# Adapter-conditioned attention with a routed low-rank layer: factor rows taken from the values' products, the last query groups crossed, first outputs in halves

## The chip, the cores and the metric
The kernel runs on one core of one Trainium2 chip. The metric is the device time of one execution in microseconds. Three runs of the kernel before gave a median of 1053.36 us (1052.51 to 1054.79).

## What is computed
`x` has 8 batches of 256 tokens with 1024 features, all in float32. Each layer of the reference adds two terms:

```python
h = x @ W.T + b + 2.0 * (x @ lora_A[a]) @ lora_B[a]      # a: one adapter per batch, rank 16
q, k, v = h @ w_q, h @ w_k, h @ w_v                      # 32 query heads, 8 key/value heads, 32 wide
o = softmax(q k^T / sqrt(32)) v                          # within a batch
x = x + o @ w_o
y = x @ weight[c].T                                      # c: one of 8 matrices per batch
logits = y @ router_w.T                                  # 4 experts, the best 2 kept, softmax
x = x + sum_e gate_e * 4.0 * (y @ A[e].T) @ B[e].T       # rank 16
```

## The kernel before, in words
Every float32 product is done as three fp32r products: each operand is split into a high part (ScalarE copies and rounds it) and a low part (VectorE subtracts), and high x high, high x low and low x high are added up in PSUM. So a `matmul` over k = 0..7 (1024 features in `KT` = 8 tiles) is 24 products.

**Fold** (`fold_stage`). `W` and `w_q`, `w_k`, `w_v` are multiplied into one matrix `wq` of twelve blocks of 128 columns (`BLOCKS`), in three chunks `j` of four blocks, and likewise `lora_B` (into `bp`, stored to DRAM as `b_scratch`) and the bias (`brow`). VectorE and ScalarE evacuate a chunk's eight tiles, split the next chunk's eight rows of `Wqkv` (`split_q`), and only then evacuate `bp`, on whose bank tile 6 of the next chunk waits.

**Attend** (`attend_stage`). Batches go in four pairs p of 512 tokens. A pair has 16 steps, one for each key/value group g = 0..7 and each batch c; N = 64 steps in all, and the work of step n is spread over steps n to n+3. In TensorE's step the order is: scores 0 and 1, **first slot** of projection products, outputs of n-3, transpose of the maxima of n-1 (`turn`), transposed scores 0 and 1 of n-2, scores 2 and 3, **second slot**, transposed scores 2 and 3 of n-2. The two slots are filled by the list `WORK`: entry s is (first slot, second slot); "q3:4-8" is k = 4 to 7 of query group 3, "+" means the next pair. The units alternate between two PSUM banks in the order `SEQ`: unit i may start (`free`) when unit i-2 has been evacuated, that is when ScalarE has written its high and VectorE its low part. VectorE finds each step's row maxima (four per step), splits them, and SP copies them as two rows into `q_stack` for the transposed scores two steps on. ScalarE takes the exponentials (four per step), GpSimd adds their halves (`p_sum`), and the outputs wait for both. Each engine and SP's DMA queue works strictly in the order written out in its `step` function.

The unit "u" is the factor h A of both batches (`project_u`): per k and batch one product with 64 weight columns and one with 32, 32 products of 256 columns a pair. It needs all of the next pair's x, so x is loaded in steps 11 and 12 as soon as q7, the last reader, lets its tiles go (`x_used`); the splits follow on ScalarE in steps 11 and 12 and on VectorE in 12 and 13. The values' units v0 to v3 (one per 128 tokens) have x as weights and 256 columns of `wq` moving, and end with one low-rank product.

**Finish** (`finish_stage`). Per batch: eight tiles `w_o_tile` of o W_o (24 products of 256 columns), `residual` on VectorE, eight rows `cond_row` (six products of 512 columns) that fold the conditional matrix into the router and A, and the gated low-rank part. What is possible is done ahead, in the last pair's steps and after (s = n - LAST, s = 0..18): `WO_LOAD` and `WO_SPLIT` load and split W_o, `load_o(0)` (nine DMAs: eight broadcast rows of reciprocal sums and o) is issued by SP in s = 8, `normalise` and `scale_lo` make o(0)'s parts on VectorE in s = 10 and 11, `FIRST_TILES` puts the eight tiles of batch 0 in the slots from the second of s = 12 on, and `ROWS_MULT` rows 0 to 4 from the second slot of s = 16 on. Rows 5 to 7, o(1)'s normalisation and tile 0 of batch 1 come in `first()`. The low part of row r needs its high part, which needs `cond_used` of row r-2; GpSimd loads rows 0 to 3 in s = 13 and the others after its last `p_sum`.

Of the kernel before, what the change touches and what calls it, by code (L numbers as in the profile page):

```python
# [32 lines left out]
BLOCKS = ["k0", "q0", "q1", "q2", "v0", "v1", "q3", "k1", "q4", "q5", "q6", "q7"]  # L33
NB = len(BLOCKS)
CHUNKS = 3
CB = NB // CHUNKS

# [12 lines left out]
WQ = BASE  # L50
SMALL = WQ + NB * 2 * D * 4
R0 = SMALL + 1024
R1 = R0 + 32768
R2 = R1 + 22528
# [13 lines left out]
def fold_stage(nc, sem, at, ctx, wq, id_sb, idx_sb, ones, W, Wqkv, bias, lora_BT, ident, idx, idx2_sb, idx2,  # L68
# [37 lines left out]
    def sync(sp, ahead):  # L106
# [12 lines left out]
        for j in range(CHUNKS):  # L119
# [9 lines left out]
            for part in range(2):  # L129
                sp.dma_start(b_scratch[part, :, cols], f(bp[:, part])).then_inc(bp_stored, 16)  # L130
# [11 lines left out]
    def scalar(act, ahead):  # L142
# [10 lines left out]
        for j in range(CHUNKS):  # L153
            if j == CHUNKS - 1:
                ahead(act, False)
            for m in range(KT):
                act.wait_ge(tile_done, KT * j + m + 1)
                nc.scalar.activation(wq[:, CB * j:CB * (j + 1), 0, m * P:(m + 1) * P],
                                     psF[:, bank(j, m)].rearrange("p (u c) -> p u c", u=CB),
                                     ACT.Copy).then_inc(tile_hi, 1)  # L160
# [6 lines left out]
            if j:  # L167
                act.wait_ge(bp_stored, 32 * j)
            nc.scalar.activation(bp[:, 0], psF[:, bank(j, 0)], ACT.Copy).then_inc(bp_hi_done, 1)
            act.wait_ge(bias_done, j + 1)  # L170
            nc.scalar.activation(brow[:], psF[0:2, bank(j, 1)], ACT.Copy).then_inc(brow_hi_done, 1)

    def vector(dve, ahead):
# [28 lines left out]
        for j in range(CHUNKS):  # L202
# [3 lines left out]
            for m in range(KT):  # L206
                dve.wait_ge(tile_hi, KT * j + m + 1)
                units, cols = slice(CB * j, CB * (j + 1)), slice(m * P, (m + 1) * P)
                dve.tensor_tensor(wq[:, units, 1, cols], psF[:, bank(j, m)].rearrange("p (u c) -> p u c", u=CB),
                                  f(wq[:, units, 0, cols]), ALU.subtract).then_inc(tile_lo, 1)  # L210
            if j + 1 < CHUNKS:
                for k in range(KT):
# [4 lines left out]
            dve.tensor_tensor(bp[:, 1], psF[:, bank(j, 0)], f(bp[:, 0]), ALU.subtract).then_inc(bp_done, 1)  # L217
# [3 lines left out]
                                     ALU.mult, ALU.subtract).then_inc(brow_done, 1)  # L221

# [75 lines left out]
SEQ = ["u", "k0", "q0", "q1", "v0", "q2", "v1", "v2", "v3", "q3", "k1", "q4", "q5", "q6", "q7"]  # L298
NS = len(SEQ)
SEQ_DVE = [u for u in SEQ if u[0] != "v"]  # L300
ND = len(SEQ_DVE)
STEPS = 2 * G
N = PAIRS * STEPS


def work(n, part):

    for w in WORK[n % STEPS][part] if n < N else []:
# [1143 lines left out]
```

## Time and profile before

| what | value |
|---|---|
| median of three runs | 1053.36 us |
| the profiled execution | 1050.59 us, span 1048.9 us |
| mean granted TensorE clock | 0.988 |
| TensorE busy | 1013.4 us, 97% |
| VectorE busy | 633.5 us, 60% |
| ScalarE busy | 449.5 us, 43% |
| GpSimd busy | 234.0 us, 22% |
| moved by DMA | 117.41 MB |

The span is the time from the first to the last instruction of one profiled execution. Fold lasts to about 162 us, attend to about 724 us with some of finish in it, and finish to the end. A product's row shows its full length with the drain of the pipeline; what a product costs is the distance to the next start.

### The profile page before, as it was taken

To read this page: it belongs to the slowest core of one execution; us is meant where nothing else is said; L and a number is where in the kernel's file an instruction comes from. 1 tells how busy PE (TensorE), PEld (TensorE's weight loads), DVE (VectorE), ACT (ScalarE), POOL (GpSimd) and SP (SyncE) were. 2 spreads that over 40 slices of the span, in tenths; PEclk is the share of its full clock that TensorE was granted. 3 is DMA by queue.
4 is the path that set the end of the run, shared out by engine and by line. 5 is a ranking of instruction groups with operands and counts; after the bars stand their busy time and mean duration, and the time that the engine had idled before them with its cause. 6 is when DMAs were issued, how large, how long until landed. Compare 5 with 4: busy or idle time off the path is not lost.

```text
span 1048.9 us, 17421 instructions
## 1 busy us (share of the span) xinstructions
PE 1013.4 (97%) x6934; PEld 820.2 (78%) x6934; DVE 633.5 (60%) x1071; ACT 449.5 (43%) x782; POOL 234.0 (22%) x224
## 2 busy tenths in 40 slices
PE   7999999999999999999999999999899999999997
PEld 6878787877678776787767787676589998988986
DVE  6562724667856578664776657654665655655653
ACT  5121223355754557554665556635422332323321
POOL 1000001123323233223332246643111111111100
PEclk9999999999999999999999999999999999999998
DMA  7030312111421124211232134453966756766531
GB/s 263 0 101 1 131 47 73 27 38 43 123 55 38 29 56 122 60 40 27 53 113 60 42 93 142 123 154 142 257 215 197 229 193 199 228 196 205 201 122 40
DMA packets 49888, 117.41 MB, mean 112 GB/s; under 512 B 7298, under 2 KB 26114, under 8 KB 45712
## 3 DMA queue, kind: packets, MB, share of 16 engines
q1 hardware_dynamic: 40080, 81.70, 26.4%
q0 software_dynamic: 9728, 34.61, 10.4%
q8 instruction: 55, 0.90, 0.4%
q14 instruction: 25, 0.20, 0.1%
HBM read 86.38 MB, written 18.89 MB: 100 GB/s over the span
## 4 chain that ended last, share of the span: by engine, by line
PE 90%; DMA 3%; DVE 3%; ACT 1%; SPq 1%; issue 1%; POOL 0%; ACTq 0%
PE psP L759 20%; PE psW L1043 17%; PE psF L254 11%; PE psG L1071 8%; PE psO L825 6%; PE psT L812 5%; PE psS L801 5%; PE psP L774 4%; PE psX L1286 3%; PE psO L829 2%; PE psY L1305 2%; PE psF L265 1%; DMA x_raw<-in_xT 1%; PE psM L836 1%; PE psP L740 1%; PE psP L742 1%
## 5 line engine op out<-in xcount | busy, mean ns | idle before, releaser
L673 DVE TENSOR_REDUCE nmax<-psS 128x2 f32<-128x512 f32 x256 | 164.5, 684 | 153.8 <-PE psS L801 152.1
L550 POOL TENSOR_TENSOR p_sum<-probs 128x512 f32<-128x512 f32 x128 | 167.6, 1310 | 372.6 <-ACT probs L600 372.3
L759 PE MATMUL psP<-x_hl,wq 128*128 128x512 f32 x960 | 235.1, 392 | 0.6 <-DVE q_stack L653 0.6
L759 PEld LDWEIGHTS psP<-x_hl,wq 128*128 128x128 f32 x960 | 175.2, 189 | 32.8 <-issue 0.8
L1043 PE MATMUL psW<-wq 128*128 128x256 f32 x1536 | 196.7, 283 | 1.6 <-DVE q_stack L653 1.2
L1043 PEld LDWEIGHTS psW<-wq 128*128 128x128 f32 x1536 | 190.3, 191 | 6.2 <-issue 1.3
L600 ACT ACTIVATE probs<-psT 128x512 f32<-128x512 f32 x256 | 139.2, 596 | 54.4 <-PE psT L812 53.9
L1052 ACT ACTIVATE cond_hi<-cond_raw 128x1024 fp32r<-128x1024 f32 x64 | 66.8, 1057 | 152.5 <-PE psG L1071 148.1
L1056 DVE TENSOR_TENSOR cond_lo<-cond_raw,cond_hi 128x1024 fp32r<-128x1024 f32 x64 | 78.3, 1235 | 89.1 <-ACT cond_hi L1052 89.0
L812 PE MATMUL psT<-q_stack,k_stack 98*128 98x512 f32 x256 | 90.1, 427 | 7.7 <-ACT probs L600 5.4
L653 DVE TENSOR_TENSOR q_stack<-psP,q_stack 32x512 fp32r<-32x512 f32 x128 | 87.8, 686 | 9.2 <-ACT q_stack L566 7.1
L801 PEld LDWEIGHTS psS<-k_stack,q_stack 96*128 96x128 f32 x512 | 80.0, 190 | 12.7 <-DVE nmax L673 1.1
L615 ACT ACTIVATE nmax_rows<-psM 16x128 f32<-16x128 f32 x64 | 17.1, 267 | 169.6 <-PE psM L836 169.6
L1003 POOL DMA_DIRECT2D cond_raw<-in_cond x64 | 33.8, 529 | 250.0 <-PE psG L1071 249.9
L801 PE MATMUL psS<-k_stack,q_stack 96*128 96x256 f32 x512 | 85.3, 287 | 0.1
L566 ACT ACTIVATE q_stack<-psP 32x512 fp32r<-32x512 f32 x128 | 75.2, 587 | 9.7 <-PE psP L766 8.1
L254 PE MATMUL psF<-q_hi,w_hi 128*128 128x512 f32 x184 | 72.0, 391 | 2.6 <-DVE bp L217 2.6
L254 PE MATMUL psF<-q_lo,w_hi 128*128 128x512 f32 x184 | 71.7, 389 | 0.0
L254 PE MATMUL psF<-q_hi,w_lo 128*128 128x512 f32 x184 | 71.6, 389 | 0.0
L825 PE MATMUL psO<-probs,v_sb 128*32 128x256 f32 x1024 | 69.3, 388 | 0.0
L812 PEld LDWEIGHTS psT<-q_stack,k_stack 98*128 98x128 f32 x256 | 43.0, 191 | 17.1 <-ACT probs L600 10.7
L825 PEld LDWEIGHTS psO<-probs,v_sb 128*32 128x32 f32 x1024 | 26.9, 110 | 31.5 <-issue 18.1
(122 smaller groups left out, 1252.8 us busy)
## 6 DMA issues: line engine op xcount, KB each, us to landing
cond_raw<-in_cond POOLq DMA_DIRECT2D x64, 512.0 KB, 4.1
x_raw<-in_xT SPq DMA_DIRECT2D x32, 256.0 KB, 3.9
q_stack<-q_stack SPq DMA_DIRECT2D x32, 256.0 KB, 3.1
o_scratch<-o_sb SPq DMA_DIRECT2D x64, 128.0 KB
o_raw<-rden_scratch SPq DMA_DIRECT2D x32, 256.0 KB, 5.4
o_raw<-o_scratch SPq DMA_DIRECT2D x8, 1024.0 KB, 8.8
x_sb<-in_xT SPq DMA_DIRECT2D x8, 1024.0 KB, 6.8
outT<-x_sb SPq DMA_DIRECT2D x32, 256.0 KB, 2.5
```

What stands on the lines that cost most here:

```text
L254: mm = pe.matmul(psF[:, bank(j, m)], w[:, k, m * P:(m + 1) * P], q[:, k], start=(k == 0 and i == 0), stop=(k == KT - 1 and i == 2))
L550: pool.tensor_tensor(p_sum[:, heads], probs[:, 0, heads], probs[:, 1, heads], ALU.add).then_inc(sum_done, 1)
L600: nc.scalar.activation(probs[:, i % 2, (i // 2) * 512:(i // 2 + 1) * 512], psT[:, i % 2], ACT.Exp, scale=ATT_SCALE).then_inc(exp_done, 1)
L653: ins = dve.tensor_tensor(to(h), both(psP[32 * h:32 * h + 32, bank(p, u)]), f(hi(h)), ALU.subtract)
L673: dve.tensor_reduce(nmax[:, n % 2, 2 * hp:2 * hp + 2, qt], psS[:, i % 2].rearrange("p (h k) -> p h k", h=2), AX.X, ALU.max, negate=True).t ...
L759: mm = pe.matmul(out, wq[:, i, w, k * P:(k + 1) * P], x[:, k, part], start=(k == 0 and n_ == 0), stop=False)
L801: mm = pe.matmul(psS[:, i % 2, j * T:(j + 1) * T], q_stack[0:96, slot, c, 2 * hp + j, qt * P:(qt + 1) * P], k_stack[0:96, c, g], start=Tru ...
L812: pe.matmul(psT[:, kt], k_stack[0:98, c, g, kt * P:(kt + 1) * P], q_stack[0:98, slot, c, 2 * hp:2 * hp + 2].rearrange("p h t -> p (h t)"), ...
L825: pe.matmul(psO[HD * h:HD * h + HD, 0], v_sb[:, c, kt, g], probs[:, kt, h * T:(h + 1) * T], start=(kt == 0), stop=(kt == KK - 1))
L1043: mm = pe.matmul(out, wq[:, k, w, m * P:(m + 1) * P], o_part(n % 2, o)[:, k], start=(k == 0 and i == 0), stop=(k == KT - 1 and i == 2))
L1056: dve.tensor_tensor(cond_lo[:, r % RAW], cond_raw[:, r % RAW], f(cond_hi[:, r % SPLIT]), ALU.subtract).then_inc(cond_lo_done, 1)
L1071: mm = pe.matmul(psG[0:EC, half], a[:, k], w[:, half * 512:(half + 1) * 512], start=(k == 0 and i == 0), stop=(k == KT - 1 and i == 2))
```

## The change
1. The unit "u" goes. The adapters' factors A stand beside the values' columns in `v_hi` (320 columns a k-tile: high and low factor of batch 1, 256 values, high and low factor of batch 0), so that the values' products move 288, 272 and 256 columns and yield the factor rows too. VectorE adds high and low (`u_tok`), TensorE turns the four token tiles (unit "t"), ScalarE and VectorE write `u_stack` from that. The values' low-rank products become units r0 and r1, which VectorE adds to `v_sb`; `v_sb` has two buffers.
2. `BLOCKS` and `WORK` are reordered: the values come first in a pair, in steps 12 to 14 of the one before, and of the last two query groups q7's first half goes before q6's second. x is loaded in three lots: four tiles in step 9, one in step 10, three in step 11 (`X_LOAD`, `X_HI`, `X_LO`). High parts of q and k are all written at the end of ScalarE's step, low parts in VectorE's next step (`late`), others at once (`soon`).
3. In the fold `bp` and `brow` are evacuated behind two of the next chunk's splits instead of eight. The last chunk's tiles are evacuated in two instructions each.
4. Finish: `load_o(0)` moves to step 14 of pair 2, o(0) is normalised and split in halves in s = 1 to 4, o(1) in s = 14 to 16; the first tiles are a slot earlier and the eighth stands in `first()` between rows 5 and 6; rows 0 to 5 are split and multiplied earlier, rows 4 and 5 loaded in s = 16.

```diff
-BLOCKS = ["k0", "q0", "q1", "q2", "v0", "v1", "q3", "k1", "q4", "q5", "q6", "q7"]
+BLOCKS = ["k0", "q0", "q1", "q2", "q3", "k1", "q4", "q5", "q6", "q7", "v0", "v1"]
...
             if j + 1 < CHUNKS:
-                for k in range(KT):
+                for k in range(2):
                     split_q(j + 1, k)
...
+            if j + 1 < CHUNKS:
+                for k in range(2, KT):
+                    split_q(j + 1, k)
...
 WORK = [
-    (["v0"], ["q2:0-4"]),
-    (["q2:4-6"], ["q2:6-8"]),
-    (["v1"], ["v2"]),
-    (["v3"], ["q3:0-4"]),
-    (["q3:4-8"], ["k1:0-4"]),
-    (["k1:4-8"], ["q4:0-3"]),
-    (["q4:3-6"], ["q4:6-8"]),
-    (["q5:0-3"], ["q5:3-5"]),
-    (["q5:5-8"], ["q6:0-3"]),
-    (["q6:3-6"], []),
-    (["q6:6-8"], ["q7:0-3"]),
-    (["q7:3-6"], []),
-    (["q7:6-8"], []),
-    (["+u:0-4"], ["+u:4-8"]),
-    (["+k0"], ["+q0"]),
-    (["+q1:0-4"], ["+q1:4-8"]),
+    (["q2:0-3"], ["q2:3-5"]),
+    (["q2:5-8", "r0"], ["q3:0-2"]),
+    (["q3:2-5"], ["q3:5-6"]),
+    (["r1", "q3:6-8"], ["k1:0-2"]),
+    (["k1:2-5"], ["k1:5-8"]),
+    (["q4:0-3"], ["q4:3-5"]),
+    (["q4:5-8"], ["q5:0-2"]),
+    (["q5:2-5"], ["q5:5-8"]),
+    (["q6:0-3"], ["q6:3-4"]),
+    (["q7:0-4"], ["q6:4-5"]),
+    (["q6:5-8"], ["q7:4-5"]),
+    (["q7:5-8"], []),
+    (["+v0:0-4"], ["+v1:0-4"]),
+    (["+v0:4-6", "+v1:4-6"], ["+v0:6-8", "+v1:6-8"]),
+    (["+v2", "+v3"], ["+t", "+k0"]),
+    (["+q0"], ["+q1"]),
 ]
+X_LOAD = {(9, 0): range(4), (10, 1): [4], (11, 0): range(5, KT)}
+X_HI = {(9, 1): range(4), (11, 0): [4], (12, 0): [5, 6], (12, 1): [7]}
+X_LO = {(10, 0): range(4), (11, 1): [4], (12, 1): [5, 6], (13, 0): [7]}
...
+        def turn_rows(p):
+            free(p, "t")
+            pe.wait_ge(proj_dve, read_unit(p, "v3") + 1)
+            for t in range(TILES):
+                mm = pe.transpose(psP[0:32, bank(p, "t"), t * P:(t + 1) * P],
+                                  u_tok[:, t].rearrange("p c r -> p (c r)"), id_sb[:])
...
+        def project_v(p, t, first, end):
...
+            hi_rows, lo_rows, lo_out = ((slice(V0, VC), slice(V0, VC - R), slice(0, NKV + R)) if c == 0 else
+                                        (slice(0, VC - V0), slice(R, VC - V0), slice(R, NKV + V0)))
+            for k in range(first, end):
...
+                pe.matmul(out[:, 0:NKV + V0], x[:, k, 0, toks], v_hi[:, k, hi_rows], start=(k == 0), stop=False,
+                          skip_group_check=True)
+                pe.matmul(out[:, lo_out], x[:, k, 1, toks], v_hi[:, k, lo_rows], start=False, stop=False,
+                          skip_group_check=True)
+                mm = pe.matmul(out[:, c * V0:c * V0 + NKV], x[:, k, 0, toks], v_lo[:, k], start=False, stop=(k == KT - 1),
+                               skip_group_check=True)
...
-    ROWS_SPLIT = {15: [0, 1], 16: [2], 17: [3, 4], 18: [5]}
-    ROWS_MULT = {(16, 1): 0, (17, 0): 1, (17, 1): 2, (18, 0): 3, (18, 1): 4}
...
+    ROWS_HI = {14: [0], 15: [1], 16: [2, 3], 17: [4], 18: [5]}
+    ROWS_LO = {(15, 0): [0], (15, 1): [1], (16, 1): [2, 3], (17, 1): [4], (18, 1): [5]}
+    ROWS_MULT = {(16, 0): 0, (16, 1): 1, (17, 1): 2, (18, 0): 3, (18, 1): 4}
+    ROWS_LOAD = {13: range(4), 16: range(4, 6)}
...
-    FIRST_TILES = {(12 + (m + 1) // 2, (m + 1) % 2): m for m in range(KT)}
+    FIRST_TILES = {place: m for m, place in enumerate([(12, 0), (12, 1), (13, 0), (13, 1), (14, 0), (14, 1), (15, 0)])}
...
-            for k in (5, 6, 7):
-                cond_row(pe, 0, k)
+            cond_row(pe, 0, 5)
+            w_o_tile(pe, 0, KT - 1, range(KT))
+            cond_row(pe, 0, 6)
+            cond_row(pe, 0, 7)
```

## Rows read from the trace of the kernel before

**Rows 1.** The page, span and busy time with share and instructions.
```profile
span 1048.9 us, 17421 instructions
...
PE 1013.4 (97%) x6934; PEld 820.2 (78%) x6934; DVE 633.5 (60%) x1071; ACT 449.5 (43%) x782; POOL 234.0 (22%) x224
```

**Rows 2.** The chain: by engine (first row), then pieces: start, length, what.
```profile
PE 90%; DMA 3%; DVE 3%; ACT 1%; SPq 1%; issue 1%; POOL 0%; ACTq 0%
...
289.08 5.46 PE psP L759 x24
...
328.98 2.87 PE psP L774 x24
...
423.51 5.46 PE psP L759 x24
...
558.90 5.46 PE psP L759 x24
```

**Rows 3.** Waits of TensorE: us in total, times, longest.
```profile
PE psG L1071 <- DVE cond_lo L1056: 6.6, 4, 3.4
PE psT L812 <- ACT probs L600: 5.4, 3, 2.3
...
PE psF L254 <- DVE bp L217: 2.6, 2, 1.4
PE psT L812 <- DMA q_stack<-nmax_rows: 2.3, 1, 2.3
PE psW L1043 <- DVE q_stack L653: 1.2, 1, 1.2
```

**Rows 4.** Windows: stretch, length, busy per engine, granted clock, DMA share, GB/s.
```profile
411.00:423.50 12.50, 10.83 (x81) 8.65 (x80) 11.25 (x19) 9.71 (x20) 3.86 (x3) 0.86 0.32 90
...
731.00:741.00 10.00, 5.76 (x36) 2.59 (x36) 2.68 (x2) 4.80 (x7) 4.43 (x6) 0.83 0.57 183
```

**Rows 5.** Timeline of TensorE, steps 13 and 14 of pair 0: start, length, operation.
```profile
286.11 0.28 PE L740 MATMUL psP<-x_hl,a_stack 128*64 128x256 f32 x1
...
287.96 0.64 PE L812 MATMUL psT<-q_stack,k_stack 98*128 98x512 f32 x2
288.43 0.65 PE L801 MATMUL psS<-k_stack,q_stack 96*128 96x256 f32 x4
...
296.13 0.28 PE L836 MATMUL psM<-id_sb,nmax_parts 128*16 128x128 f32 x1
296.17 0.72 PE L812 MATMUL psT<-q_stack,k_stack 98*128 98x512 f32 x2
296.72 0.65 PE L801 MATMUL psS<-k_stack,q_stack 96*128 96x256 f32 x4
```

**Rows 6.** Groups by line and shape: busy us, mean ns | idle before.
```profile
L550 POOL TENSOR_TENSOR p_sum<-probs 128x512 f32<-128x512 f32 x128 | 167.6, 1310 | 372.6 <-ACT probs L600 372.3
L673 DVE TENSOR_REDUCE nmax<-psS 128x2 f32<-128x512 f32 x256 | 164.5, 684 | 153.8 <-PE psS L801 152.1
...
L653 DVE TENSOR_TENSOR q_stack<-psP,q_stack 32x512 fp32r<-32x512 f32 x128 | 87.8, 686 | 9.2 <-ACT q_stack L566 7.1
```

**Rows 7.** Timeline of SP's queue and ScalarE, third reload of x.
```profile
537.57 1.50 SPq L424 DMA_DIRECT2D x_raw<-in_xT  x3
...
547.01 0.63 ACT L428 ACTIVATE x_hl<-x_raw 128x512 fp32r<-128x512 f32 x1 [0.80 <-DMA x_raw<-in_xT]
```

**Rows 8.** Timeline of TensorE, a step whose second slot is empty.
```profile
391.52 0.65 PE L801 MATMUL psS<-k_stack,q_stack 96*128 96x256 f32 x4
...
393.65 1.55 PE L759 MATMUL psP<-x_hl,wq 128*128 128x512 f32 x6
```

**Rows 9.** Timeline of TensorE, behind the last pair's wait for the maxima.
```profile
670.64 3.43 PE L759 MATMUL psP<-x_hl,wq 128*128 128x512 f32 x9
```

**Rows 10.** Timeline of GpSimd, step 11 of the last pair.
```profile
681.61 3.36 POOL L550 TENSOR_TENSOR p_sum<-probs 128x512 f32<-128x512 f32 x1 [0.19 <-ACT probs L600]
```

**Rows 11.** Timeline of ScalarE, high part of row 4.
```profile
737.90 1.06 ACT L1052 ACTIVATE cond_hi<-cond_raw 128x1024 fp32r<-128x1024 f32 x1 [4.39 <-DMA cond_raw<-in_cond]
```

More of the change, by code:

```diff
@@ L221, in vector @@
                                      ALU.mult, ALU.subtract).then_inc(brow_done, 1)
+            if j + 1 < CHUNKS:
+                for k in range(2, KT):
+                    split_q(j + 1, k)
     def tensor(pe):
@@ L395, in bank, with factor @@
         return unit(p, u) % 2
+    def factor(c, low):
+        i = (NKV + V0 + low * R) if c == 0 else (1 - low) * R
+        return slice(i, i + R)
     def pair_rows(scratch, p):
@@ L486, in step @@
             more = n < N and p + 1 < PAIRS
-            if more:
-                for k in {11: range(0, 3), 12: range(6, KT)}.get(s, ()):
-                    load_x(sp, p + 1, k)
             if 1 <= n <= N:
@@ L495, in step @@
                                  nmax_rows[8 * part:8 * part + 8, (n - 1) % 2]).then_inc(rows_landed[(n - 1) % 2], 16)
-            if more and s == 11:
-                for k in range(3, 6):
+            if more:
+                for k in X_LOAD.get((s, 0), ()):
                     load_x(sp, p + 1, k)
-            for unit_ in evacuated(n, 0):
+            ahead.sync(sp, n, 0)
+            for unit_ in soon(n, 0):
                 double(*unit_)
@@ L510, in step @@
                 store_rden(sp, p - 1)
-            for unit_ in evacuated(n, 1):
+            if more:
+                for k in X_LOAD.get((s, 1), ()):
+                    load_x(sp, p + 1, k)
+            for unit_ in late(n):
                 double(*unit_)
@@ L951, in load_x, with ahead_sync @@
         sp.dma_start(x_sb[:, n % 2], xT[n]).then_inc(x_landed[n % 2], 16)
-    def ahead_sync(sp, n):
+    def ahead_sync(sp, n, part):
         s = n - LAST
+        if part == 0:
+            if s == -2:
+                sp.wait_ge(before.proj_done, unit(PAIRS - 1, "v3") + 1)
+                for i in range(2):
+                    sp.wait_ge(before.o_stored[i], 32 * G)
+                load_o(sp, 0)
+            return
         for k in WO_LOAD.get(s, ()):
@@ L957, in ahead_sync @@
             sp.dma_start(wo_raw[:, k, 1], Wo[k * P:(k + 1) * P]).then_inc(wo_landed[k], 16)
-        if s == 8:
-            sp.wait_ge(before.proj_done, unit(PAIRS - 1, "q5") + 1)
-            for i in range(2):
-                sp.wait_ge(before.o_stored[i], 32 * G)
-            load_o(sp, 0)
         if s == 11:
@@ L1097, in ahead_vector @@
             residual(dve, 0, m)
-        if part == 1 and s == 14:
+        if part == 1 and s == 13:
             dve.wait_ge(ra_hi_done, 1)
             dve.tensor_tensor(ra_lo[:], ra_raw[:], f(ra_hi[:]), ALU.subtract).then_inc(ra_lo_done, 1)
-        if part == 1:
-            for r in ROWS_SPLIT.get(s, ()):
-                cond_row_lo(dve, r)
+        if part == 1 and s == 14:
+            normalise(dve, 1)
+        for r in ROWS_LO.get((s, part), ()):
+            cond_row_lo(dve, r)
+        if part == 0 and s == 16:
+            scale_lo(dve, 1)
     def ahead_gpsimd(pool, n):
```

380 lines of the change are left out of this document (212 added, 168 removed).

## The prediction, made before the change was timed
> **What bounds the kernel now.** I read the page's busy times first: TensorE is busy in 97% of the span, the next engine (VectorE) in 60%, so time is won only where TensorE has fewer products to do or waits less [rows 1]. The chain that ended last says the same: 90% of it is TensorE's [rows 2]. TensorE's waits come next [rows 3]. Of some 31 us only a few places lie in reach of this change: 6.6 us for lows of conditional rows, 5.4 us in three waits for exponentials, 2.6 us for `bp`, 2.3 us for a DMA of row maxima, 1.2 us for the last queries' lows. [...] Behind the last pair's wait for the row maxima nine 512-column products take 3.43 us, drain included, where 9 x 0.2275 is 2.05 [rows 2, 9]; over the tail's longest wait the mean grant is 0.83 [rows 4]. What a pair boundary loses shows best as a period: k0 of pair 1 starts at 289.08, of pair 2 at 423.51, of pair 3 at 558.90, so the periods are 134.4 and 135.4 us [rows 2].
>
> **TensorE's own work.** A product of 512 columns costs 5.46 / 24 = 0.2275 us and one of 256 columns 2.87 / 24 = 0.1196 us [rows 2]; between them a column costs 0.42 ns. The low-rank factor products (L740, L742) run at the same 256-column price although their weights are narrower: sixteen in 1.85 us, 0.116 us each [rows 5]. Thirty-two per pair go, 128 in all: 15.0 us less. The values' products stay at 96 per pair, but a third of them widen to 288 columns and a third to 272: 48 columns for each three products, 128 triples, 6144 columns, by 0.42 ns: 2.6 us more. That width is in no row. Its bounds are 0 (256 columns happen to cover the weight load) and the price of 512 columns, 256 x 0.108 = 27.6 us; I take the straight line, since both ends of it are rows of this trace and 288 lies close to the lower. The values' low-rank products are moved out of their group (r0, r1), the same sixteen in all, at no change. Four transposes a pair (t) are new. The one transpose in each step starts 0.04 us before its successor and makes that pair of products 0.55 instead of 0.47 us long [rows 5]: 0.12 us, so 16 x 0.12 = 2.0 us; bounds 0.6 (issue alone) and 16 x 0.2275 = 3.6 us (a 512-column product's price). Sum: 15.0 - 2.6 - 2.0 = **10.4 us less**. In pair 0 nothing lies between the values' fourth tile and its transpose but the reduction on VectorE, so there t waits: **0.5 us more** (0.2 to 1).
>
> **Fold.** TensorE waits twice, 2.6 us together, because `bp` is split behind eight splits of the next chunk [rows 3]. With only two of them ahead, `bp` is ready some 4 us sooner, while six tiles of the next chunk (18 products, 4.1 us) run ahead of the one that needs it: the wait goes, **2.6 us less**. Splits 2 to 7 come later but are needed 5.5 us apart. The last chunk's doubled evacuations (sixteen for eight) are covered by 5.5 us of `lora_B` products. The cost, were that cover gone, is about 3 us.
>
> **Pair boundaries.** The first half of a step with k0 lasts 288.43 to 296.72, less k0's 25 products (5.69) 2.60 us; the second half has two more groups of 0.47 [rows 5]: 3.55 us of base. The plain work of a period before is sixteen of these, ten q/k units of 5.69, four value tiles of 2.99, u at 3.7: 129.4 us; after, by the prices above, 126.8. So the rows of the periods hold 5.0 and 6.0 us of loss; for the first boundary, with the shortest wait, I take 4.5. It consists of the wait for exponentials, the low clock behind it (0.86 over 12.5 us around the second boundary [rows 4]), and steps with an empty second slot, which cost 2.13 instead of 1.42 us for the same three groups [rows 8]: 0.7 us each. Why the wait: SP issues three x tiles from 537.6 on, two rows, then three more, and ScalarE, in order as the queue is, has the sixth only at 547.0, 9.4 us after the first issue, with the next step's exponentials queued behind [rows 7].
>
> After the change four tiles are issued in one lot in step 9, behind the two row DMAs, 1.3 us after the transpose. By the old lots (six tiles, two rows between, within 9.4 us) four tiles take about 6 us to land. That puts ScalarE's last split some 6 us into step 10, where its row copy and exponentials are wanted at 4.5 to 6 us. So the wait moves from step 12 to step 10 and shrinks to about 1 us, plus 0.8 us of slip while the next exponentials are worked off one by one. Next late is VectorE: its step costs four maxima at 0.68 (two and two, 2.6 us) and 0.9 for their parts, and 2.8 us of lows when a query group was finished [rows 6], and steps 10, 11 and 12 now carry q6's lows, q7's lows and seven x lows of the same width. That is 3 x 3.5 + 2 x 2.8 + 7 x 0.68 = 21 us against 18.9 us of TensorE. v1 in step 12 needs the bank that q7's lows free: about 1.1 us. v2 in step 14 needs v0 reduced and copied: 0.45 us. With 0.7 us for the one empty slot left and half a chance of the low clock (2 us) this is 5.05 us per boundary; some of the waits lie in each other's shadow (v1's behind step 10's), and I take 4.6. The three boundaries give back 15.5 - 3 x 4.6 = **1.7 us less**; with no stall at all it would be 13.7, and at 8 us each 8.5 us more.
>
> **Last pair.** `load_o(0)`, nine DMAs, leaves the SP queue ahead of the row maxima of step 9; the 2.3 us wait goes and with it 1.2 us of low clock [rows 3, 9]. It moves to step 14 of pair 2, which lasts 15.7 us; behind it in SP are one store and k0's copy, needed a step later. W_o tiles in both slots of step 12 cover q7's lows (1.15 us) and p_sum (1.1 us), and one empty slot less is 0.7 us: 6.5 us. Against it, normalise and low part of o(0) join the lows on VectorE in steps 2 and 4, 7.5 us against 6.3 and 7.9: 1.2 us. **5.3 us less** (bounds 2 and 6.5).
>
> VectorE's `scale_lo` beside a p_sum (2.3 us) made that p_sum 3.36 us long instead of 1.31 [rows 6, 10]. The Trainium skill (SBUF, "Who interferes with whom") has the rule: a VectorE instruction with two SBUF inputs and a GpSimd one that reads SBUF exclude each other for a whole instruction. By it each of the four half operations in steps 1 to 4 could hold a p_sum for 1.15 us and each whole one in steps 14 and 16 for 2.3 us, 9 us in all if every one hit TensorE. The sum takes 1 us of it, in step 16 alone, because elsewhere a W_o tile or a projection stands between.
>
> **Tail.** Row 3's low is 3.4 us late since its high waits behind the last exponentials, and three more lows are late by 3.2 us together [rows 3], among them row 4's, whose load waits behind the last p_sum (ScalarE idle 4.4 us [rows 11]), and one behind the normalising of o(1). With 0.5 us for o(1)'s split and some 1.3 us of low clock behind the longest (grant 0.83 over 731 to 741, 5.76 us of it busy [rows 4]) that is 8.4 us. Rows 0 to 3 a slot or more sooner, rows 4 and 5 loaded in step 16, o(1) ready in step 16, tile 7 between rows 5 and 6 (2.87 us of cover): most of it goes. New: the second slot of step 15 is empty and row 0 waits for the last maxima (1.1), p_sum (1.0), rows 4 and 5 right behind the last outputs (1.7). **4.6 us less** (bounds 1 and 8).
>
> **Sum.** 10.4 - 0.5 + 2.6 + 1.7 + 5.3 + 4.6 = 24.1 us. The profiled execution took 1050.6 us (span 1048.9), so 1026.5 in its terms; the median of the runs is 2.8 us above it, 1053.36, so **1029.3 us** is forecast.
>
> **Rivals.** (a) *The reload hides wholly*: x lands sooner and VectorE's backlog is taken up by step 13, the boundaries lose only their empty slot, the last pair and the tail lose 1 us together. 10.4 - 0.5 + 2.6 + 13.7 + 6.5 + 7.5 = 40.2, 1013 us. For it: 5 us of light steps follow each lot; against it: ScalarE takes no exponential until the lot is in. (b) *The reload bites more*: four tiles take 7 us, ScalarE's first exponentials of step 10 are 2.4 us late as at the third boundary (part of the 5.4 us in [rows 3]), and two low-clock stretches follow: 8 us per boundary, 1040 us. (c) *The rows' work returns as a wait*: reduction, copy and transpose in series hold TensorE 2.6 us per pair, and the change to u is worth nothing: 1040 us. This is the case where the change doesn't do what it says; against it, v2 and v3 together are 6 us long and k0 5.7 us. (d) *Slower*: the new shapes are dear. If 288 and 272 columns cost what 512 do and a transpose 0.23 us, TensorE gains 15.0 - 27.6 - 3.6 = -16.2 instead of 10.4, and the sum is 2.5 us on the other side: 1056 us. It decides from a widened product of about 0.22 us on.
>
> **How the numbers follow.** Forecast 46 in 100, (a) 20, (b) 18, (c) 10, (d) 4, and 2 for a result within 0.2% by several small misses. A measurement of this kernel tells about 0.2% (2 us) from no change. All but (d) and the last are faster: 0.94, 0.02, 0.04. The range reaches to (a) and past (b) and (c): 1013 to 1042; what is left out is (d), and the outer half of (a) and a little of (b), 15 to 20 in 100.
>
> **What would show it.** Right: L740 and L742 gone, values' triples 0.38 us apart, no wait for `bp`, none for row maxima behind `load_o`, first tail wait under 1.5 us, k0-to-k0 periods near 131 us (126.8 + 4.6), with the wait for exponentials now in step 10. Wrong: periods near 127 (a) or 135 (b), a wait at t (c), or triples over 0.6 us (d). [...]

## The result, and the profile after

The changed kernel takes 1025.41 us (median of 4 runs, 1024.67 to 1028.63), the kernel before on the same chip 1054.07 (1052.51 to 1057.24): a ratio of 0.973, 95% interval 0.9699 to 0.9761. Against the median that I predicted from (1053.36) that is 28.0 us less; forecast were 24.1 less, 1029.3 us, and the range was 1013 to 1042. The profiled execution of the changed kernel is its slowest, 1028.63 us (span 1027.0), 22.0 less than the profiled one of before (1050.59). All accounts below are made between these two profiles.

From the page of the changed kernel, its span, busy times and the chain by engine; they answer to [rows 1, 2].

```profile
span 1027.0 us, 17259 instructions
...
PE 998.8 (97%) x6822; PEld 806.7 (79%) x6822; DVE 640.3 (62%) x1101; ACT 447.1 (44%) x786; POOL 234.5 (23%) x224
...
PE 89%; DVE 4%; DMA 3%; ACT 1%; SPq 1%; issue 1%; POOL 0%; POOLq 0%; ACTq 0%
```

TensorE is the bound as before. Its waits (us in total, times, longest) answer to [rows 3]:

```profile
PE psT L896 <- ACT probs L645: 3.2, 3, 1.5
PE psP L840 <- DVE q_stack L703: 3.1, 3, 1.0
PE psG L1165 <- DVE cond_lo L1150: 1.3, 2, 0.9
PE psS L885 <- DVE nmax L734: 1.3, 2, 0.8
PE psX L1388 <- DVE g_t L1311: 1.1, 1, 1.1
...
PE psS L885 <- issue: 1.0, 3, 0.4
PE psO L909 <- ACT probs L645: 0.9, 1, 0.9
```

The waits for `bp` (2.6) and for the maxima's DMA (2.3) are gone, the lows of the conditional rows fell from 6.6 to 1.3. The three waits for exponentials at L896 fell only from 5.4 to 3.2, and three for q7's lows (L840) and two for maxima (L885) are new.

The new shapes, from the timeline of TensorE in step 14 of pair 0 and before k0 of pair 1 (start, length, operation; 128x288 is the width moved):

```profile
287.32 0.29 PE L840 MATMUL psP<-v_hi,x_hl 128*128 128x288 f32 x1
...
287.69 0.30 PE L840 MATMUL psP<-v_hi,x_hl 128*128 128x288 f32 x1
...
294.39 0.60 PE L802 MATMUL psP<-id_sb,u_tok 128*32 128x128 f32 x4
294.75 1.63 PE L818 MATMUL psP<-x_hl,wq 128*128 128x512 f32 x6
```

Triples start 0.37 us apart (287.32, 287.69) where 0.38 was forecast, and the four transposes take 0.36 us (294.39 to 294.75) where I had 0.5.

The periods, from the chain of the changed kernel (start, length, what); they answer to [rows 2]:

```profile
294.99 5.49 PE psP L818 x24
...
428.05 5.48 PE psP L818 x24
...
561.62 5.49 PE psP L818 x24
```

They are 133.1 and 133.6 us, against 134.4 and 135.4 before and 131.4 forecast. To see where the 2 us are I took each step's length from the starts of its first scores, less its products at the prices of the prediction and less the 3.55 us that a step's other work (scores, outputs, transposes) takes. In most steps of both kernels that leaves less than 0.05 us; what is left in the others is loss (us, boundary 1 / 2 / 3):

| | before | after |
|---|---|---|
| steps 9 to 11 | 1.2 / 1.2 / 1.2 | 2.0 / 4.1 / 4.6 |
| steps 12, 13 | 4.0 / 4.0 / 4.9 | 1.4 / 1.4 / 1.4 |
| steps 14, 15 and the next step 0 | 0 / 0 / 0 | 1.0 / 1.0 / 1.0 |
| sum | 5.2 / 5.2 / 6.1 | 4.5 / 6.5 / 6.9 |

So the boundaries lose 17.9 us where they lost 16.5: 1.4 more, and 1.7 less was forecast. Step 11 has the one empty second slot that the change leaves. Step 10 of pair 1 in the changed kernel, timeline of all engines:

```profile
385.48 1.31 SPq L536 DMA_DIRECT2D q_stack<-nmax_rows  x2
386.84 1.98 SPq L470 DMA_DIRECT2D x_raw<-in_xT  x4
...
389.71 0.63 ACT L474 ACTIVATE x_hl<-x_raw 128x512 fp32r<-128x512 f32 x1 [1.55 <-DMA x_raw<-in_xT]
391.42 0.63 ACT L474 ACTIVATE x_hl<-x_raw 128x512 fp32r<-128x512 f32 x1 [1.08 <-DMA x_raw<-in_xT]
392.49 1.21 ACT L474 ACTIVATE x_hl<-x_raw 128x512 fp32r<-128x512 f32 x2 [0.43 <-DMA x_raw<-in_xT]
393.76 1.05 ACT L645 ACTIVATE probs<-psT 128x512 f32<-128x512 f32 x2
394.38 0.97 PE L896 MATMUL psT<-q_stack,k_stack 98*128 98x512 f32 x2 [1.03 <-ACT probs L645]
```

The lot (four tiles of x) is issued behind the rows, ScalarE is held by it until 393.7, 4.9 us after its last issue, and the exponentials come behind. What the clock takes after such waits is in the windows (stretch, length, busy per engine, grant, DMA share, GB/s):

```profile
256.00:263.76 7.76, 7.15 (x52) 4.67 (x51) 5.72 (x11) 5.12 (x11) 2.44 (x3) 1.00 0.50 153
...
395.20:403.50 8.30, 8.27 (x49) 5.62 (x49) 6.11 (x11) 5.02 (x12) 2.58 (x3) 0.79 0.30 82
```

Pair 0's wait is 0.61 us and the grant is 1.00 in the step in which it lies (first row) and in the next one. Behind the wait of 1.03 us it is 0.79 over the whole of step 11 (second row), and again 0.79 over 528.8 to 537.0 behind the wait of 1.5: a part of those stretches ran at 1.2 GHz, and the two steps lose 1.6 us more each than pair 0's. Two such losses are 0.003 of the whole execution's grant. This execution has a mean grant of 0.992; the other three have 0.996, 0.996 and 0.995 and are 3.0 to 4.0 us shorter. So they can't have had both stretches: the low clock at the boundaries belongs to this execution more than to the median.

### The profile page after: what moved, and what is told of

Same layout as the page of the kernel before. It is cut to its first block, busy times and chain, and to the rows that moved or that the text cites. A ratio compares the mean times of both kernels' runs of the same rounds, so it can differ in the third digit from the quotient of the medians.

```text
span 1027.0 us, 17259 instructions
## 1 busy us (share of the span) xinstructions
PE 998.8 (97%) x6822; PEld 806.7 (79%) x6822; DVE 640.3 (62%) x1101; ACT 447.1 (44%) x786; POOL 234.5 (23%) x224
## 4 chain that ended last, share of the span: by engine, by line
PE 89%; DVE 4%; DMA 3%; ACT 1%; SPq 1%; issue 1%; POOL 0%; POOLq 0%; ACTq 0%
PE psP L818 20%; PE psW L1137 17%; PE psF L280 12%; PE psG L1165 8%; PE psO L909 5%; PE psS L885 5%; PE psT L896 5%; PE psX L1388 3%; PE psO L913 2%; PE psY L1407 2%; PE psF L291 2%; PE psP L840 2%; DVE nmax L734 1%; DMA x_raw<-in_xT 1%; DVE q_stack L703 1%; PE psP L842 1%
## 5 line engine op out<-in xcount | busy, mean ns | idle before, releaser
L818 PE MATMUL psP<-x_hl,wq 128*128 128x512 f32 x960 | 239.9, 395 | 0.2 <-DVE v_sb L724 0.2
L885 PEld LDWEIGHTS psS<-k_stack,q_stack 96*128 96x128 f32 x512 | 78.9, 189 | 17.5 <-issue 2.9
L896 PE MATMUL psT<-q_stack,k_stack 98*128 98x512 f32 x256 | 88.7, 423 | 3.2 <-ACT probs L645 3.2
L885 PE MATMUL psS<-k_stack,q_stack 96*128 96x256 f32 x512 | 85.4, 286 | 2.5 <-DVE nmax L734 1.3
L896 PEld LDWEIGHTS psT<-q_stack,k_stack 98*128 98x128 f32 x256 | 43.1, 191 | 12.3 <-ACT probs L645 7.8
```

Of the source, the lines that this page charges most:

```text
L818: mm = pe.matmul(out, wq[:, i, w, k * P:(k + 1) * P], x[:, k, part], start=(k == 0 and n_ == 0), stop=False)
L885: mm = pe.matmul(psS[:, i % 2, j * T:(j + 1) * T], q_stack[0:96, slot, c, 2 * hp + j, qt * P:(qt + 1) * P], k_stack[0:96, c, g], start=Tru ...
L896: pe.matmul(psT[:, kt], k_stack[0:98, c, g, kt * P:(kt + 1) * P], q_stack[0:98, slot, c, 2 * hp:2 * hp + 2].rearrange("p h t -> p (h t)"), ...
```

## Experiments

All are timed beside the kernel before. Ratios are to it, with 95% intervals; "the changed kernel" was timed a second time among them.

**1. The changed kernel again.** No edit.

> The changed kernel itself, unaltered, beside the others on one chip, to tell what differs by the edit from what differs from one execution to the next. Expected: the same median as before within 0.3%, so 1022 to 1028, and from the two profiles of this one program how far the waits and the stretches at the low clock repeat: the waits of step 10 for exponentials (0.61, 1.03, 1.5 us) should stand again within 0.3 us, since they come from SyncE's queue; if the low clock follows each wait above 1 us, it stands in the same places, and if it is drawn by chance, it doesn't.

Measured: 1026.61 us (1023.76 to 1032.17), ratio 0.9746 (0.9716 to 0.9776). The step table repeats: step 10 loses 0.8, 1.6 and 2.0 us (1.2, 1.6, 2.1 in the first profile), step 11 0.8, 2.4 and 2.4, with the low clock in the same two places. So the waits belong to the schedule, but for pair 0's, which is 0.3 us this time. The low clock behind them doesn't come in every execution. Both profiled executions have a mean grant of 0.992. Of the ten executions of this kernel, the five at 0.995 or 0.996 take 1023.8 to 1025.7 us, and the five at 0.989 to 0.993 take 1026.1 to 1032.2. So two profiles with the low clock in the same places don't show that the schedule brings it each time.

**2. x issued ahead of the rows** (`x_first`).

```diff
         def step(n):
+            if more:
+                for k in X_LOAD.get((s, 0), ()):
+                    load_x(sp, p + 1, k)
             if 1 <= n <= N:
...
-            if more:
-                for k in X_LOAD.get((s, 0), ()):
-                    load_x(sp, p + 1, k)
             ahead.sync(sp, n, 0)
```

> The changed kernel (1025.4 us) with SyncE's order turned round: the lots of x's tiles are issued ahead of the rows' transfers of the same step. Theory: step 10 loses 1.2 to 2.1 us a pair because x lands late (pair 1: the rows' issue stands ahead at 385.48, x's four issues follow at 386.84 with 1.98 each, ScalarE starts on x_hl at 389.71 and the exponentials come last to the products), and the low clock behind the waits of 1.03 and 1.5 us costs another 1.6 in step 11 of pairs 1 and 2. With x issued some 1.4 us earlier the waits for exponentials in step 10 go below 0.3 and the low clock with them: 4 to 7 us less than the changed kernel, 1018.5 to 1021.5. Rival: what holds ScalarE is x's transfer itself (1.9 us) and the buffer that VectorE frees late, not the order of the queue: the same as the changed kernel, 1024.5 to 1026. Second rival: the rows, 1.4 us later each, become what the scores wait for: slower than the changed kernel by 1 to 3 us.

Measured: 1022.09 us (1019.64 to 1024.71), ratio 0.9708 (0.9679 to 0.9736), 2 to 4 us less than the changed kernel by the ratios, whose intervals overlap; the profiles are clear. SyncE and ScalarE in the same step as above:

```profile
380.89 2.56 SPq L470 DMA_DIRECT2D x_raw<-in_xT  x4
384.89 1.32 SPq L539 DMA_DIRECT2D q_stack<-nmax_rows  x2
...
387.46 2.19 ACT L474 ACTIVATE x_hl<-x_raw 128x512 fp32r<-128x512 f32 x4
391.16 0.27 ACT L663 ACTIVATE nmax_rows<-psM 16x128 f32<-16x128 f32 x1 [1.51 <-PE psM L920]
```

x is issued 5.9 us sooner, 5.3 us sooner in its step (not 1.4, as I expected: SyncE had waited for the rows to be written; and the 1.98 us that the expectation gives to each issue is the time of all four), ScalarE splits all four tiles without a wait and then has 1.5 us to spare. Step 10 loses 0.03, 0.05 and 0.04 us in place of 1.2, 1.6 and 2.1, step 11 0.7, 0.8 and 0.6. From step 0 of pair 0 to that of the last pair it takes 385.0 us against 393.9: 8.9 us less. Of these, 3.2 are the two low-clock losses in step 11, which half of the executions of the changed kernel can't both have had. The spans of the two profiles differ by only 5.3 us, since a low clock turns up in the tail of this one (720 to 730: 0.78) where the changed kernel's had none. Executions of like grant are the fair comparison: at 0.995 to 0.997 this kernel takes 1019.6 to 1020.6 us and the changed one 1023.8 to 1025.7 (on other chips), about 5 us less. The order of the queue, and nothing in the transfer itself, made the wait.

**3. The lot cut in two** (`two_and_two`).

```diff
-X_HI = {(9, 1): range(4), (11, 0): [4], ...
-X_LO = {(10, 0): range(4), (11, 1): [4], ...
+X_HI = {(9, 1): [0, 1], (10, 0): [2, 3], (11, 0): [4], ...
+X_LO = {(10, 0): [0, 1], (10, 1): [2, 3], (11, 1): [4], ...
```

> The changed kernel with the first lot of x's tiles cut in two: ScalarE copies tiles 0 and 1 in the slot as before and tiles 2 and 3 a slot later (VectorE's remainders likewise), so it stands for two tiles between two exponentials instead of four. Theory (ScalarE held by the lot is what makes the exponentials late): the waits for exponentials in step 10 (0.61, 1.03, 1.5 us) and the low clock behind the last two go, 3 to 6 us less than the changed kernel, 1019.5 to 1022.5. Rival: the remainders moved to the next slot make VectorE late in steps 11 and 12, and the wait comes back there: 1024 to 1027. If it is the landing of x alone and not the number of tiles, the wait for tile 0 stays and so do the times: 1024.5 to 1026.

Measured: 1021.97 us (1020.65 to 1025.31), ratio 0.9708 (0.9683 to 0.9733). Step 10 loses 0.06, 0.04 and 0.6 us; step 11 rises to 1.4, 1.6 and 1.6 (0.8 where no low clock disturbed it), and a new wait of up to 0.9 us appears for q6's doubling DMA, whose lows VectorE writes behind the postponed remainders. Step 12 loses 0.8 to 1.0 instead of 1.4. Theory and rival are both seen; on balance it is worth what `x_first` is. The wait needs both: a lot that lands late, and exponentials behind the whole of it.

**4. v1 behind a longer v0** (`x_v05`, with the edit of 2).

```diff
-    (["+v0:0-4"], ["+v1:0-4"]),
-    (["+v0:4-6", "+v1:4-6"], ["+v0:6-8", "+v1:6-8"]),
+    (["+v0:0-5"], ["+v1:0-4"]),
+    (["+v0:5-6", "+v1:4-6"], ["+v0:6-8", "+v1:6-8"]),
```

> The changed kernel with x's tiles issued ahead of the rows' transfers (as in x_first) and, beside it, the first slot of step 12 made one column tile of x longer (v0 tiles 0 to 4 there and v1 tiles 0 to 3 behind it, v0's sixth and seventh in step 13), so that the value products of v1 start 1.1 us later behind q7's lows, for which they wait 1.0 us a pair. Theory: the wait goes, 3 x 1.0 less than x_first, which lies 2 below the changed kernel: 1017.5 to 1020.5. Rival: VectorE's lows move too, since its work of step 12 is released by the longer slot, and the wait stays: 1021 to 1023.

Measured: 1019.31 us (1018.43 to 1021.79), ratio 0.9682 (0.9654 to 0.9709); on the same chip that is 7.3 below the changed kernel. v1's first product in step 12 of pair 0, TensorE's timeline:

```profile
276.03 0.37 PE L840 MATMUL psP<-v_hi,x_hl 128*128 128x288 f32 x1 [0.64 <-DVE q_stack L703]
```

The wait falls from 1.03 to 0.64, not to nothing, and steps 12 and 13 lose 0.9, 0.7 and 0.9 us instead of 1.2, 1.1 and 1.3. So a third of the theory's 3 us came: from step 0 of pair 0 to that of the last pair it is 383.8 us, 1.2 less than in `x_first`. That the median still fell into the theory's range is luck: three of the six executions of `x_first` have a mean grant of 0.992, and only two of these five lie under 0.995. Above that it is 1018.4 to 1019.3 us here and 1019.6 to 1020.6 there, 1.2 less again. VectorE's maxima and lows are released by the same step, and move with it, as the rival says.

**5. The load of o(0) late again** (`load_o_late`; its scaling, normalising and splitting go back with it).

```diff
-            if s == -2:
...
-                load_o(sp, 0)
...
+        if s == 8:
+            sp.wait_ge(before.proj_done, unit(PAIRS - 1, "q5") + 1)
...
+            load_o(sp, 0)
...
+        if part == 0 and s == 10:
+            normalise(dve, 0)
+        if part == 1 and s == 11:
+            scale_lo(dve, 0)
```

> The changed kernel with one edit undone: the last outputs' data for the first half are loaded in step 8 of the last pair again instead of ahead of step -1, and normalised and scaled in steps 10 and 11. Theory: behind that load on SyncE's queue the rows of step 9 come late, and what the kernel before showed comes back: a wait of about 2.3 us for the rows with 1.2 at the low clock behind it, 3 to 4 us more than the changed kernel, 1028.5 to 1029.5. Rival (the wait before was due to the row maxima being late for another reason, which the other edits removed): the same as the changed kernel, 1025 to 1026.

Measured: 1037.19 us (1032.87 to 1038.75), ratio 0.9849 (0.982 to 0.9877): 11 to 13 us more than the changed kernel, not 3 to 4. SyncE's queue in the last pair (the last issues of the load, then the rows), and TensorE's instructions with a wait:

```profile
647.47 1.72 SPq L1033 DMA_DIRECT2D o_raw<-rden_scratch  x4
649.23 0.42 SPq L1035 DMA_DIRECT2D o_raw<-o_scratch  x1
651.37 1.32 SPq L536 DMA_DIRECT2D q_stack<-nmax_rows  x2
```

```profile
660.56 0.77 PE L896 MATMUL psT<-q_stack,k_stack 98*128 98x512 f32 x2 [2.96 <-DMA q_stack<-nmax_rows]
670.87 0.98 PE L896 MATMUL psT<-q_stack,k_stack 98*128 98x512 f32 x2 [1.07 <-ACT probs L645]
673.60 3.10 PE L1136 MATMUL psW<-wq 128*128 128x256 f32 x24 [1.27 <-issue]
```

The rows are issued at 651.37, 2 us behind the megabyte of `o_scratch`, and are there only at 660.5. The place and the kind of wait are the theory's. The size isn't: steps 10 to 12 lose 7.1 us more than in the changed kernel, since the exponentials (1.07) and the W_o tile (1.27) come late behind the first wait, which its own step's low clock follows (0.87 over 653 to 664). The tail loses another 3 us, with a grant of 0.83 over 730 to 750; that this comes from the load isn't shown, since `x_first` has such a stretch in its tail too.

**6. Rows 4 and 5 late again** (`rows_late`).

```diff
-    ROWS_LOAD = {13: range(4), 16: range(4, 6)}
+    ROWS_LOAD = {13: range(4)}
...
-            load_cond(pool, n, range(6, KT) if n == 0 else range(KT))
+            load_cond(pool, n, range(RAW, KT) if n == 0 else range(KT))
```

> The changed kernel with rows 4 and 5 of the first gating loaded only behind the last sum of probabilities, so that the tail finds them later. Theory: they have little slack (the first gate's products wait 0.9 us in the tail now), so 1 to 4 us more than the changed kernel, 1026.5 to 1029.5. Rival: the tail is held by GpSimd's sum and the outputs' halves, and the rows have slack: same as the changed kernel, 1025 to 1026, or 0.5 to 1 less, since GpSimd issues less ahead of its sums.

Measured: 1031.76 us (1029.53 to 1035.05), ratio 0.9808 (0.9779 to 0.9836), 6 to 8 us more than the changed kernel. GpSimd's issue, ScalarE's high part of row 4, and TensorE's wait for its low part:

```profile
713.06 2.26 POOL L1093 DMA_DIRECT2D cond_raw<-in_cond  x4
...
717.02 1.06 ACT L1146 ACTIVATE cond_hi<-cond_raw 128x1024 fp32r<-128x1024 f32 x1 [5.26 <-DMA cond_raw<-in_cond]
...
719.39 1.12 PE L1165 MATMUL psG<-cond_hi,ra_hi 128*68 128x512 f32 x2 [5.58 <-DVE cond_lo L1150]
```

The theory's mechanism, at 5.6 us instead of 1 to 4, and a grant of 0.78 over the 11 us behind it.

**7. The fold's order alone** (`fold_only`, the kernel before with part 3's first edit, on both engines).

```diff
-                for k in range(KT):
+                for k in range(2):
                     split_q(j + 1, k)
...
+            if j + 1 < CHUNKS:
+                for k in range(2, KT):
+                    split_q(j + 1, k)
```

> The kernel before (1053 us) with one edit of the change alone: in the folding stage ScalarE and VectorE split only two of the next chunk's tiles ahead of the bias product's copies and the other six behind them. Theory: TensorE's wait of 2.6 us for that copy goes and the stretch at the low clock behind it gives up to 0.7 more, so 2.6 to 3.3 us less than the kernel before, 1050 to 1050.5. Rival: the six splits put behind the copies make the next chunk's products wait instead: within 0.5 us of the kernel before.

Measured: 1049.18 us (1045.97 to 1056.33), ratio 0.9965 (0.9944 to 0.9987), so 1.4 to 5.9 less. The wait for `bp` is gone and none has come: the first group of TensorE's groups over the fold, of before and then of this kernel (busy us, mean ns | idle before):

```profile
L254 PE MATMUL psF<-q_hi,w_hi 128*128 128x512 f32 x184 | 72.0, 391 | 2.6 <-DVE bp L217 2.6
```
```profile
L260 PE MATMUL psF<-q_hi,w_hi 128*128 128x512 f32 x184 | 71.8, 390 | 0.0
```

From the group's first product to the first scores it is 165.9 us against 169.2: 3.3 less. The grant over the fold of before is 1.00, so the 0.7 above the wait isn't the low clock that I named; it stays unexplained.

**8. The factor products left out of the kernel before** (`u_one`: column tiles 1 to 6 of eight).

```diff
             for k in range(first, end):
                 pe.wait_ge(x_lo_done, KT * p + k + 1)
+                if k not in (0, KT - 1):
+                    continue
```

> The kernel before with 96 of the 128 products of x with the low-rank factors left out (column tiles 1 to 6 of each unit's eight, so the low-rank part of queries, keys and values is that of two tiles alone and the outputs aren't the reference's). Theory (these products lie on TensorE's path and nothing else is late behind them): 96 x 0.117 = 11.2 us less than the kernel before, 1041.5 to 1042.5. Rival (what waits behind them, the copies of the low-rank rows and the values' halves, is late anyway and the time comes back as waits): 0 to 5 us less, 1048 to 1053.

Measured: 1055.38 us (1050.87 to 1057.03), ratio 1.0012 (0.9995 to 1.0028): nothing is gained. Step 13 of pair 0, ScalarE, then TensorE:

```profile
277.35 2.39 ACT L566 ACTIVATE q_stack<-psP 32x512 fp32r<-32x512 f32 x4
279.76 1.08 ACT L600 ACTIVATE probs<-psT 128x512 f32<-128x512 f32 x2
...
281.10 1.94 PE L827 MATMUL psO<-probs,v_sb 128*32 128x256 f32 x16 [2.29 <-ACT probs L600]
```

ScalarE works q7's highs ahead of the exponentials. In the kernel before, 16 factor products (1.86 us) stand in the slot ahead of the outputs and cover that. With 12 of them gone the outputs wait 2.29 us (1.58 and 2.14 at the next two boundaries), the grant over 277 to 287 is 0.66, and step 13 lasts 9.65 us instead of 9.11 (8.2 and 9.1 instead of 8.7 and 9.1 at the next two). My theory fell, and the rival's wait was another than the one it named.

**9. Only the second slot's** (`u_second`).

```diff
+                if k in (4, 5, 6):
+                    continue
```

> The kernel before with 48 of the 128 products of x with the low-rank factors left out, all in the second slot of step 13 (column tiles 4 to 6; the low-rank part is then that of five tiles, and the outputs aren't the reference's). The first slot's 16 products stay. When 96 were left out, in both slots, nothing was gained: in step 13 of pair 0 the outputs then waited 2.29 us for the exponentials 279.76, which stand on ScalarE behind q7's highs (277.35, 2.39), and the low clock followed. Theory (the products of the first slot, 1.86 us, only cover that wait; those of the second cover nothing): 48 x 0.117 = 5.6 us less than the kernel before, a ratio of 0.993 to 0.996. Rival (all of step 13 is held by ScalarE, or what is left out comes back behind the u products as a wait at k0 for the low-rank rows, as in the prediction's third rival): 0 to 1 us less.

Measured: 1048.31 us (1045.69 to 1054.84), ratio 0.9956 (0.9937 to 0.9975), 4.6 less. Step 13 lasts 7.6, 7.4 and 8.4 us in the three boundaries instead of 9.1, 8.7 and 9.1; twelve products at 0.117 us are 1.4, and in two boundaries of three all of it comes. Half as many products are left out as in run 8, and they count. What TensorE's work is worth depends on the slot that it leaves: in one slot it is the cover for ScalarE, in the other it is time. (A kernel without the first slot's alone wasn't run.)

**10. The gates' copies first** (`turn_first`, with the edits of 2 and 4).

```diff
-                if m == 7 and n == 0:
-                    turn_copies(n)
...
                     before.invert(dve, PAIRS - 1)
+                    turn_copies(n)
                 if m == 6 and n == 0:
```

> x_v05 (1019.3 us) with one more edit in the tail: VectorE copies the turned gates ahead of the second factor's remainder (1.22 us) instead of behind it. Theory: TensorE's wait for those copies (1.14 us at 731.39 of the changed kernel) falls to 0.2 to 0.8, since the transposes end only at about 730.2: 0.4 to 0.9 us less than x_v05, and up to 2 more in executions in which the low clock follows that wait (722.98 of x_first: 4.74 for 32 products that take 3.79 at full clock). Rival: the remainder, later by 0.8, makes the low-rank products of the first gating wait: the same or up to 0.5 more.

Measured: 1019.13 us (1018.52 to 1020.71), ratio 0.9681 (0.9654 to 0.9708). The wait falls from 1.2 us in the profile of `x_v05` to 0.63; by the medians it is 0.2 us, which can't be told from none.

The kernels of 4 and 10 are the fastest here, 3.2% below the kernel before and 0.5 to 0.7% below the changed one.

## Why the prediction came out as it did

The total was right within 4 us. As a sum of seven terms it held partly by luck, since errors of both signs cancel. Term by term, between the two profiles (us less):

| term | forecast | measured |
|---|---|---|
| TensorE's work (2.77 a pair at the new prices) | 10.4 | 11.1 |
| t in pair 0 waits | -0.5 | -0.4 |
| fold | 2.6 | 3.3, and 0.5 from an earlier start |
| boundaries | 1.7 | -1.4 |
| ramp of pair 0 | 0 | -1.9 |
| last pair | 5.3 | 5.6 |
| tail | 4.6 | 5.5 |
| sum | 24.1 | 22.3 (spans: 21.9) |

**TensorE's work.** The straight line between the 256- and the 512-column price held (0.377 a triple), so rival (d) with its dear shapes is out. The transposes were the mis-sized part, 1.4 us for sixteen instead of 2.0: four side by side don't each cost what one among longer products does. But the forecast took for granted that a product taken away is time gained. Runs 8 and 9 show that this holds for half of the factor products only, in the kernel before. In the changed kernel the work's 11.1 us come in full, as the step lengths show. I put that down to the value products that stand where the factor products stood, and to q7's highs, which are no longer ahead of step 13's exponentials; no run shows it.

**Boundaries.** This is the term that came out with the wrong sign. The mechanism and the place were right (the wait for exponentials in step 10), and for this profile so was the size: I put the wait at 1 us, and it is 0.6, 1.0 and 1.5. With 0.8 of slip, 0.7 for the empty slot and half a chance of 2 us of low clock, steps 10 and 11 were to lose 3.5 us a boundary, 10.5 in all; they lose 1.2 + 1.6 + 2.1 and 0.8 + 2.5 + 2.4, 10.6. That the clock's part agrees is luck: it came in two boundaries of three, 1.6 us each, in the execution that was profiled, while by their mean grants half of the executions can't have had both. The 4.1 us by which the boundaries' loss exceeds the 13.8 forecast lie elsewhere. Step 12, where v1 waits for q7's lows, loses 1.4 for the 1.1 forecast (0.9 more in three boundaries). The 0.45 that I took off because the waits would lie in each other's shadow didn't come off (1.3 more): v1 waits 1.0 us in every boundary, also behind the longest wait of step 10. And I hadn't seen that step 15 and the step 0 behind it lose 0.6 us per boundary (1.8 more). On the other side the loss of the kernel before was 16.5, where I had 15.5. The 0.6 us come, it seems, from q0's doubling DMA, for which the first scores of the new pair need to wait: q0 comes to ScalarE last in the step now ("high parts of q and k are all written at the end"). The view below names no releaser, but the copy is issued at 313.10 and such copies take 2.9 to 3.2 us to land here, so until 316.0 to 316.3:

```profile
310.68 2.40 ACT L610 ACTIVATE q_stack<-psP 32x512 fp32r<-32x512 f32 x4
313.10 0.58 SPq L524 DMA_DIRECT2D q_stack<-q_stack  x1
...
316.42 0.71 PE L885 MATMUL psS<-k_stack,q_stack 96*128 96x256 f32 x4 [0.36 <-issue]
```

The landing estimate itself was near: by the old lots I had four tiles take 6 us. The third is there 5.7 us after the first issue (386.84 to 392.49), and the fourth by 393.1, when ScalarE goes on without a wait. What I didn't ask is why the lot should be issued behind the rows at all; run 2 shows that this order costs 8.9 us of the profile, low clock included, and about 5 us of an execution without it.

**Ramp.** The change moves the lows of a query group ahead of the maxima of pair 0's first steps, and I didn't cost that. Step 1's scores wait for them (start, length; VectorE, then TensorE), step 3's as well (0.47):

```profile
190.92 2.79 DVE L703 TENSOR_TENSOR q_stack<-psP,q_stack 32x512 fp32r<-32x512 f32 x4
193.74 1.29 DVE L734 TENSOR_REDUCE nmax<-psS 128x2 f32<-128x512 f32 x2
194.57 1.01 PE L885 MATMUL psS<-k_stack,q_stack 96*128 96x256 f32 x4 [0.82 <-DVE nmax L734]
```

**Last pair.** 5.6 for 5.3. Run 5 shows that the load's place carries the whole of it, and that in the new schedule it is worth twice the 2.3 + 1.2 us of the old one (7.1 us in steps 10 to 12), since more comes late behind it. The term held because it was read from the old schedule's own waits, which are what the change took away.

**Tail.** 5.5 for 4.6. Of the three losses that I put at new places, the 1.1 us at the last maxima is 0.3, the 1.0 at p_sum is 0.59 and the 1.7 at rows 4 and 5 is 0.44 + 0.89. Not in the sum was 0.9 us in which the last outputs wait for exponentials. The p_sums there are long beside VectorE's `normalise` and `scale_lo` (VectorE's and GpSimd's timeline, start, length):

```profile
695.93 2.29 DVE L1103 TENSOR_TENSOR o_raw<-o_raw 128x2048 f32<-128x2048 f32 x1 [1.62 <-DMA o_raw<-o_scratch]
696.27 3.09 POOL L596 TENSOR_TENSOR p_sum<-probs 128x512 f32<-128x512 f32 x1 [2.52 <-ACT probs L645]
...
701.71 1.28 POOL L596 TENSOR_TENSOR p_sum<-probs 128x512 f32<-128x512 f32 x1 [2.35 <-ACT probs L645]
...
705.87 2.29 DVE L1113 TENSOR_TENSOR wq<-o_raw,wq 128x2048 fp32r<-128x2048 f32 x1 [0.31 <-ACT wq L1109]
707.09 3.44 POOL L596 TENSOR_TENSOR p_sum<-probs 128x512 f32<-128x512 f32 x2 [2.61 <-ACT probs L645]
```

3.09 us for one sum beside `normalise`, 1.28 for one alone, 3.44 for two beside `scale_lo`: the first stands until VectorE is done (698.2) and then takes its own 1.1. TensorE felt it once, 0.59 us behind the pair at 707.09. This trace agrees with the rule of the Trainium skill (SBUF — State Buffer, "SBUF: two separate sides") that of such a pair the one that starts first has the shared port for its whole instruction. Run 6 shows that the early load of rows 4 and 5 carries the whole term: late, it costs 5.6 us in one wait.

**Between the runs.** In terms of the profile the forecast was 1026.5, and 1028.6 came: 2.1 too low. In terms of the median it was 3.9 too high. The 6.0 us between lie in which execution was profiled: I carried over that the median of before lies 2.8 us above its profile, and the changed kernel's lies 3.2 below its own (run 1: one program takes 1023.8 to 1032.2 us, with mean grants of 0.996 to 0.989). Most of these 3.2 us are the two low-clock losses, which the other three executions can't both have had.

**Rivals.** (a) needed boundaries that lose only an empty slot; `x_first` shows that the reload can hide, but not as the change issues it. (b) would be 8 us a boundary; 6.9 is the worst. (c) has its place refuted, t waits in pair 0 alone; its general form, that the removed work was cover, is true of the kernel before (run 8). The one thing under "what would show it" that came out wrong is the period: 133.1 and 133.6 lie between forecast (131) and (b) (135).

## What to carry to other kernels

Price a removed product by its slot: look at what the engine ahead of the next wait is doing meanwhile, since a product may be nothing but its cover. When a transfer is moved, check in which order its queue issues it: an instruction that stands behind one which waits for a result of the same step goes out that much later, and one such order put a transfer off by 5 us here. Waits near 1 us on a TensorE that is otherwise full are worth removing first, since the low clock behind them can take more than they do (1.6 us behind 1.03 here). And before a difference between two profiles is put down to the edit, compare the mean grants of all executions: which low-clock stretches a profile holds is part of the draw.

## What the runs showed of the hardware

The granted clock can fall after a wait of about 1 us. In the changed kernel's profile 1.03 and 1.5 us are followed by 0.79 over a step, 0.61 by 1.00. The length of the wait alone doesn't decide. In the kernel before, the wait of 1.39 us for exponentials at 278.5 is followed by 0.81 over 278.4 to 287.5, while the wait of 1.4 us for `bp` [rows 3] is followed by none (1.00 over 14 to 183). In the changed kernel the 1.03 us for q7's lows in step 12 is followed by nothing, and behind the wait for the gates' copies 32 products take 3.79 us in the changed kernel (1.14 us of wait) and 4.74 in `x_first` (0.94 us), grant 0.78 over 720 to 730. At the boundaries it stands in the same two places in both profiles of the changed kernel, but the mean grants (0.989 to 0.996) say that other executions of the same program have less of it or more. What decides stays open.

```profile
722.98 4.74 PE L1388 MATMUL psX<-g_t,x_sb 128*128 128x68 f32 x32 [0.94 <-DVE g_t L1311]
```
```profile
731.39 3.79 PE L1388 MATMUL psX<-g_t,x_sb 128*128 128x68 f32 x32 [1.14 <-DVE g_t L1311]
```

In `load_o_late` two rows of 4 KB were issued 2 us behind a transfer of 1 MB on the same queue, and TensorE waited for them until 660.5, 9 us after their issue (651.37).
